# Unit 3's first token-mixing layer and its normalisations on GpSimd instead of VectorE, under a new plan of the instruction order

## The reference

```python
x = x + gated_scan(_layernorm(x))      # i, f, o = sigmoid(x@W+b), s = tanh(x@W+b); h = f*h + i*s; then o*h + x, normalised, *gamma + beta
x = x + mixing(_layernorm(x))          # the first token-mixing layer
x = x + attention(_layernorm(x))       # 16 heads of 16 channels, causal over 4096 tokens
x = x + mixing(_layernorm(x))          # the second token-mixing layer

def mixing(x):
    x_prev = x shifted by one token
    xr = mu_r * x + (1.0 - mu_r) * x_prev
    xk = mu_k * x + (1.0 - mu_k) * x_prev
    return sigmoid(xr @ W_r.T) * (square(relu(xk @ W_k.T)) @ W_v.T)
```

## Time and profile before

| | |
|---|---|
| median of 3 runs | 1678.7 us (1675.02 to 1678.71) |
| profiled execution, its own time | 1679.5 us |
| its span in the profile | 1677.8 us, granted clock 0.994 of full speed |
| TensorE busy | 1625.4 us, 97% |
| VectorE busy | 1511.0 us, 90% |
| ScalarE busy | 1308.5 us, 78% |
| GpSimd busy | 940.3 us, 56% |

### The profile page before, as it was taken

One profiled execution on the slowest core, in us unless ns is written; L12 is line 12 of the kernel. 1 busy time (PEld: TensorE's weight loads), 2 busy tenths in 40 slices (PEclk: granted clock), 3 DMA queues, 4 the chain that ended last, 5 costly groups with the idle time before them and its releaser, 6 DMA issues.

```text
span 1677.8 us, 50396 instructions
## 1 busy us (share of the span) xinstructions
PE 1625.4 (97%) x20458; PEld 663.6 (40%) x20458; DVE 1511.0 (90%) x2905; ACT 1308.5 (78%) x2590; POOL 940.3 (56%) x1295
## 2 busy tenths in 40 slices
PE   8999999999999999999999999999999999999997
PEld 6656444444434344343443332333333332332214
DVE  6868998988999999999999999999999999999603
ACT  2535587667778877888878888988888999888994
POOL 3358878897995798768584534553523520425101
PEclk9999999999999999999999999999999999999999
DMA  4143223113122121131130110103110000000000
GB/s 110 46 90 59 50 56 61 47 42 63 46 45 52 33 52 31 28 57 40 31 59 10 27 33 8 32 19 66 20 25 9 25 8 20 15 14 15 9 1 14
DMA packets 127767, 61.59 MB, mean 37 GB/s; under 512 B 78512, under 2 KB 127536, under 8 KB 127536
## 3 DMA queue, kind: packets, MB, share of 16 engines
q1 hardware_dynamic: 125296, 57.33, 15.7%
q10 hardware_dynamic: 2240, 1.05, 0.4%
HBM read 25.31 MB, written 16.52 MB: 25 GB/s over the span
## 4 chain that ended last, share of the span: by engine, by line
PE 46%; DVE 41%; ACT 5%; POOL 4%; issue 4%; DMA 1%; ACTq 0%; POOLq 0%; DVEq 0%
DVE span_max L2088 34%; PE psum L2442 13%; PE psum L2397 8%; PE psum L2421 8%; PE psum L2168 4%; PE psum L2178 4%; PE psum L2149 3%; PE psum L2157 2%; ACT probs L1744 2%; DVE span_max L2082 1%; ACT probs L1733 1%; DVE small L1930 1%; DVE rows L2020 1%; PE psum L2451 1%; PE psum L2404 1%
## 5 line engine op out<-in xcount | busy, mean ns | idle before, releaser
L2088 DVE TENSOR_REDUCE span_max<-psum 128x1 f32<-128x512 f32 (+1 forms) x2048 | 1237.0, 672 | 35.1 <-PE psum L2397 28.1
L1733 ACT ACTIVATE probs<-psum 128x512 f32<-128x512 f32 (+3 forms) x1788 | 881.1, 568 | 173.0 <-PE psum L2421 169.7
L2397 PE MATMUL psum<-k_stack,q_stack 48*128 48x512 f16 (+3 forms) x2304 | 570.8, 364 | 8.8 <-DVE span_max L2088 5.3
L2421 PE MATMUL psum<-q_stack,k_stack 50*128 50x512 f16 (+3 forms) x2304 | 542.5, 364 | 8.9 <-ACT probs L1744 2.5
L2442 PE MATMUL psum<-probs,v_aug 128*17 128x512 f32 (+3 forms) x3968 | 486.1, 562 | 5.2 <-POOL probs L1569 3.8
L2421 PEld LDWEIGHTS psum<-q_stack,k_stack 50*128 50x128 f16 x2304 | 149.1, 93 | 399.9 <-ACT probs L1733 222.6
L2397 PEld LDWEIGHTS psum<-k_stack,q_stack 48*128 48x128 f16 x2304 | 168.7, 93 | 250.1 <-DVE span_max L2088 165.3
L1569 POOL TENSOR_SCALAR_AFFINE_SELECT probs<-probs 128x512 f32<-128x512 f32 x116 | 74.3, 644 | 182.5 <-ACT probs L1744 115.1
L1733 ACT ACTIVATE w_gates<-psum 128x512 f32<-128x512 f32 (+1 forms) x254 | 130.7, 573 | 17.0 <-PE psum L2421 16.8
L2442 PEld LDWEIGHTS psum<-probs,v_aug 128*17 128x17 f32 x3968 | 67.9, 95 | 119.5 <-issue 96.7
L1562 POOL TENSOR_TENSOR rows<-rows 128x512 f32<-128x512 f32 x26 | 33.2, 1275 | 141.0 <-ACT rows L1674 141.0
(11 more groups left out here) (242 smaller groups left out, 1905.3 us busy)
## 6 DMA issues: line engine op xcount, KB each, us to landing
q_stack<-q_parts SPq DMA_DIRECT2D x192, 32.0 KB, 2.0
k_stack<-k_parts SPq DMA_DIRECT2D x42, 128.0 KB, 4.8
rows<-in_x SPq DMA_DIRECT2D x16, 256.0 KB, 2.9
q_parts<-rows SPq DMA_DIRECT2D x32, 128.0 KB, 1.9
...
```

The costliest lines, as they stand in the source:

```text
L1733: act.activation(probs_of(tile)[:, i, q0:], bank(b)[:, q0:], ACT.Exp, scale=SCALE / QK_SCALE).then_inc(exp_done, 1)
L2088: nc.vector.tensor_reduce(span_max[:, s % SPAN_RING, row:row + 1, k0 // SPAN:k0 // SPAN + 1], bank(b)[:, 0:k1 - k0], AX.X, ALU.max).then_i ...
L2397: ins = nc.tensor.matmul(bank(b)[:, at:at + k1 - k0], q_stack[row:row + SCORE_ROWS, s % Q_RING, v, qt * P:(qt + 1) * P], k_stack[row:row + ...
L2421: nc.tensor.matmul(bank(b)[:, q0:], k_stack[row:row + STACK, g * PAIRS + u, j * P:(j + 1) * P], q_stack[row:row + STACK, s % Q_RING, u, q0 ...
```

## The change

One condition is changed, so that unit 3 leaves VectorE: its four layer norms (before the scan, inside it, before the mixing layer and before the attention) and its first mixing layer. The gated scan of unit 3 stays on VectorE.

```diff
 EARLY = 4
+MIXED_FROM = 3
 LATE = 2
...
 def at_ends(u, ln):
-    return u >= UNITS - LATE if ln == LAST else u < EARLY
+    return u >= UNITS - LATE if ln == LAST else u < MIXED_FROM
```

```diff
-         "dve": (-0.708182031, -15.8951964, 1.56327716, 3.03122896, 3.00215546, 3.03122896, 1.71856018, 2.60387184,
+         "dve": (3.63918768, 1.79871535, 1.79871535, 1.57086866, 7.61597661, 5.55265664, 1.74462935, 1.97922519,
...
-    "DVE": {"ao.scale": 860, "g.max": 602, "g.clip": 75, "h.clip": 1170, "h.scale": 4415, "g.scale": 1890, "qk.scale": 1680, "w.lo": 662, "ones.late": 200, "ln.stats": 660, "ln.mean": 154, "is": 602, "scan": 1615, "y": 671, "z": 600, "mixk": 790, "mixr": 790,
-            "r*kv": 605, "q.part1": 790, "kk.part1": 790, "x3": 600, "neg": 175, "part0": 90, "part1": 195,
-            "recip": 164, "norm": 331, "halve": 300, "prepare": 1950, "halve.v": 336, "scale.bound": 2870, "scale.apply": 2800,
+    "DVE": {"ao.scale": 860, "g.max": 602, "g.clip": 75, "h.clip": 1170, "h.scale": 4415, "g.scale": 1890, "qk.scale": 1680, "w.lo": 760, "ones.late": 200, "ln.stats": 660, "ln.mean": 154, "is": 602, "scan": 1800, "y": 850, "z": 600, "mixk": 950, "mixr": 950,
+            "r*kv": 605, "q.part1": 790, "kk.part1": 790, "x3": 600, "neg": 175, "part0": 260, "part1": 300,
+            "recip": 164, "norm": 331, "halve": 300, "prepare": 1950, "halve.v": 336, "scale.bound": 2870, "scale.apply": 2800,
...
-LANDS_AT = {("store_x2", 1): 5500, ("store_x2", 2): 6500, ("x1.turn", 4): 5200, ("load_q", 0): 3600, ("load_q", 1): 3600}
+LANDS_AT = {("store_x2", 1): 3500, ("store_x2", 2): 4000, ("x1.turn", 4): 4000, ("load_x", 5): 5500, ("load_x", 6): 3500,
+            ("load_q", 0): 6500, ("load_q", 1): 5500, ("load_q", 2): 3800, ("shift.turn", 1): 3500}
```

```diff
-                        sp.wait_ge(spilled_shift, 16 * (s - 1))
+                        sp.wait_ge(spilled_shift[s % 2], 16 * (s // 2))
```

More of the change, by code:

```diff
@@ L236 @@
     "SP": {"ff.turn": 2480, "a.turn": 2480, "load_ao": 500, "load_r": 500, "load_kf": 500, "load_vf": 500, "units.late": 200, "x1.turn": 2480, "x3.turn": 2480, "load_x": 500, "store_x2": 500, "store_q": 1000, "store_k": 1000, "load_k": 2800, "load_q": 2550,
-           "load_x2": 500, "store_out": 500, "shift.turn": 1300, "shift.spill": 400, "place": 900}}
+           "load_x2": 500, "store_out": 500, "shift.turn": 1150, "shift.spill": 400, "place": 700}}
 TURNED = 1300
 LANDS = {"ff.turn": TURNED, "a.turn": TURNED, "load_ao": 5000, "load_r": 5000, "load_kf": 5000, "load_vf": 5000, "units.late": 2500, "x1.turn": 2300, "x3.turn": TURNED, "load_x": 2700, "store_x2": 2200, "store_q": 2000, "store_k": 2000, "load_k": 6200, "act.load_k": 3500,
-         "load_q": 2400, "load_x2": 2700, "store_out": 2200, "shift.turn": 1300, "shift.spill": 1900, "place": 2200}
+         "load_q": 2400, "load_x2": 2700, "store_out": 2200, "shift.turn": 1500, "shift.spill": 1300, "place": 1400}
 PRODUCT = 650
@@ L1010, in build @@
             sem(n) for n in ("squared", "sums_read", "clipped", "powered", "w_scaled", "w_qk_scaled", "w_hi", "w_lo"))
-        a_lo, a_turned, ao_loaded, ao_scaled = (sem(n) for n in ("a_lo", "a_turned", "ao_loaded", "ao_scaled"))
+        a_lo, a_turned, ao_loaded = (sem(n) for n in ("a_lo", "a_turned", "ao_loaded"))
         hi_ready = sem("hi_ready")
@@ L1050, in build @@
         span_reduced = sem("span_reduced")
-        neg_ready, part_ready, shift_ready, turned_shift, spilled_shift = (
-            sem(n) for n in ("neg_ready", "part_ready", "shift_ready", "turned_shift", "spilled_shift"))
+        neg_ready, part_ready, shift_ready = (sem(n) for n in ("neg_ready", "part_ready", "shift_ready"))
+        turned_shift, spilled_shift = ([sem(f"{n}_shift{b}") for b in range(2)] for n in ("turned", "spilled"))
         shift_placed = [sem(f"shift_placed{b}") for b in range(2)]
@@ L1824, in _ @@
                         ins = nc.vector.tensor_scalar(cols[:, COL[name], :], cols[:, COL[name], :], by, None, ALU.mult)
-                    ins.then_inc(qk_scaled, 1)
+                    ins.then_inc(raw_scaled, 1)
                 elif op[0] == "ones.late":
@@ L1887, in _ @@
                 elif op[0] == "qk.scale":
-                    dve.wait_ge(qk_scaled, 1)
+                    dve.wait_ge(raw_scaled, 1)
                     settle(nc.vector.reciprocal(w_power[:, PLAIN:PLAIN + 2], qk_scale))
@@ L1899, in _ @@
                     nc.vector.tensor_scalar(weights["aq"][:], weights["aq"][:], v_back, None,
-                                            ALU.mult).then_inc(ao_scaled, 1)
+                                            ALU.mult).then_inc(raw_scaled, 1)
                 elif op[0] == "w.lo":
@@ L2099, in _ @@
                     if s >= 2:
-                        dve.wait_ge(turned_shift, 16 * (s - 1))
+                        dve.wait_ge(turned_shift[s % 2], 16 * (s // 2))
                     if s == 0:
@@ L2297, in _ @@
                         if u == 0:
-                            pe.wait_ge(qk_scaled, 1)
+                            pe.wait_ge(raw_scaled, 1)
                         if u == SPLIT_FROM:
@@ L2340, in _ @@
                         else:
-                            pe.wait_ge(ao_scaled, 1)
+                            pe.wait_ge(raw_scaled, 2)
                             pe.wait_ge(aT_ready, u - (UNITS - LATE) + 1)
```

69 lines of the change are left out of this document (36 added, 33 removed), and 99 rows, old and new, of the table WORTH.

## The result

The kernel after takes 1698.7 us (median of 4 runs, 1696.45 to 1700.23) against 1678.7 for the one before: ratio 1.0126, 95% interval 1.0112 to 1.0139, slower by 20 us. I had forecast 1671, and the range ended at 1690. The profiled executions lie 17 us apart (1696.45 and 1679.5), their spans 16.6.

What follows compares the result with a forecast made beforehand. VectorE and TensorE were both taken as nearly full, with GpSimd's pace setting VectorE's wait at chunk 2. 1679.5 + 5 - 4 - 9 = 1671.5 on the profiled execution, so 1671 us against the median; range 1657 to 1690.

Steps and rivals of the forecast that it cites:

- +5 at chunk 2: At the 161st reduction, chunk 2's first: 5 us late, from GpSimd's 5 and TensorE's 3, which do not add.
- GpSimd's 5: From 117 us to the 161st reduction: GpSimd's 144.2 us of work with 6% gaps needs 153.4, late by about 5.
- The second place of the order: At the 49th reduction, chunk 1's first: no later than 176 us, with unit 3's keys just ahead of it.
- -4 given back behind chunk 2: Behind the 161st reduction: TensorE has 7 us less to do, of which 4 reach the end.
- -9 from waits that a better plan removes: VectorE's 28.1 us of waits for maxima scores: corrected planner costs remove a third, 9 us, from between 0 and 20.
- 14 would prove me wrong: Between 265.8 and 558 us: the forecast is wrong if the waits for scores stay at 14 us.
- the tail: Behind the last reduction: should stay 98 us, with the same matmuls there; the forecast is wrong if it moves.
- VectorE's lighter start: Ahead of the first reduction: 7.1 us of VectorE's work leave, counted as 0 gain with a bound of 7.
- The fourth rival: Between 117 and 265.8 us: GpSimd holds up VectorE's two-input work, 5.6 us; 1682 us, chance 0.08.
- The third: At the 161st reduction: GpSimd becomes the bound for chunk 2, 15 us late, 4 back; 1687 us, chance 0.20.
- Theory B: Experiments' hypothesis, whole kernel: the new order costs the time; the move alone stays within 6 us of before.

Runs made afterwards that it cites:

- new_order_vector: The kernel after in its own order, but unit 3's norms and first mixing layer back on VectorE: 1698.6 us.
- earlier_49th: The kernel after with pieces moved ahead in its order: chunk 1's first query load, first four scores for maxima and their reductions: 1702.6 us.
- more_tensor: 192 repeated matmuls added in unit 7's gate products, between the 49th and 161st reductions: 1705.8 us on the kernel after, 1692.8 on the kernel before.
- short_unit6: The kernel after with unit 6's gate products on 16 of 256 columns: 1698.2 us.
- four_jobs_behind: The kernel before with four TensorE jobs (96 matmuls) moved from ahead of the 161st reduction's first score to behind the 169th score: 1683.4 us.
- eight_jobs_behind: The kernel before with eight TensorE jobs (192 matmuls) moved from ahead of the 161st reduction's first score to behind the 169th score: 1690.1 us.

## Why the prediction was wrong, step by step

Between the two profiled executions the sum was +5 - 4 - 9. The traces have +17.8 at the 161st reduction, +0.4 from there to the last and -1.6 behind it: 16.6 us.

**"+5 at chunk 2" was mis-sized: 17.8, and its larger part is the term that I had made small.** I had priced TensorE's jobs that are pulled ahead of the 161st at 7 us, taken off 4 for idle time that the new plan would fill, and then let it vanish behind GpSimd's 5. TensorE's busy time up to the 161st grew by 15.7 us, and its idle time did not shrink but grew from 17.8 to 19.9: nothing was filled. Some 3.5 us of the 15.7 are the net loss of the clock, so about 12 are jobs that I had priced at 7. Busy time is not work alone, so the 12 are no more than near: behind the 161st TensorE has 158 matmuls less on record and the same busy time (1294). With unit 3 on VectorE in the new order it is the same (busy for 17.9 more).

**GpSimd's 5 rested on a misread wait.** I took VectorE's 4.15 us ahead of the 161st for GpSimd's pace. SyncE had issued the keys' load by 253.3 us, and stood for VectorE's own shifts. GpSimd's work from 117 us to the 161st was priced well (145.0 us for 144.2, by the windows view of 117 to 283.7), and its gaps were 13%, not the 6% that I chose. Yet VectorE does not wait for its keys at that place in either kernel, and new_order_vector, without unit 3 on GpSimd, has the 161st at 285.0.

**A step without a term in the sum.** The second place of the order showed that all 48 reductions of chunk 0 would stand ahead of unit 3's keys. I drew from it only that the 49th "should come no later than 176 us". Behind a unit's keys come their store, their load and the load of queries; with no reductions left, VectorE must stand through most of that. It did: 20.4 us from the keys' end (162.5) to the 49th, 10.1 of them idle, and the 49th at 182.9. A price stood in the earlier trace rows, 17.6 us from 248.2 to 265.85, though 5.2 of that were SyncE's wait for VectorE. This gap is where 6.6 of the 17.8 us are first seen, but it is not by itself the loss: earlier_49th closed 5.8 us of it and gained nothing. Three things end there nearly together: the loads, VectorE's own queue, and TensorE, which from the first reduction to the 49th is busy for 7.2 us more than before and idle for 0.9 only (3.5 before).

What share each has of the 17.8 us is not settled. Work added to TensorE is felt nearly in full (more_tensor), but work taken from it brought nothing (short_unit6, four_jobs_behind, eight_jobs_behind), and less of GpSimd's brought 5.0 us, most of them by way of TensorE's clock.

**"-4 given back behind chunk 2": nothing came back.** From the 161st to the last reduction the kernel before takes 1313.3 us and after 1313.7, and all kernels with either order in place behind the 161st take 1312 to 1318, whatever was lost ahead of it. TensorE's 7 us less to do there bought nothing. The reason stands in the windows view: VectorE is busy for 1279 us of these 1314 in both kernels, with the same reductions, so less work of TensorE has next to nothing to shorten. And 192 more matmuls ahead of it in the old order were paid nearly in full.

**"-9 from waits that a better plan removes": none.** Over the whole span the waits for scores, masked ones counted in both, rose from 33.6 to 45.6 us. Between 265.8 and 558 us they are 14.1 us, where I had said that 14 would prove me wrong; by the same count they were 16.4 there before. One wait did go, the 4.15 us ahead of the 161st, and others came. Costs nearer to the measured ones did not make a better plan here.

**Right:** VectorE's work (-8.6 for -9.4), GpSimd's (+14.9 for +17.8), nearly the tail (96.2 for 98, though I had said it would stay), and that VectorE's lighter start gains nothing: the first reduction is at 119.8 us after 117.8, which also misses the 110 to 117 that I had named. The fourth rival's price did not come either: the 30 scans by line 2020 took 946 ns on average after 1063. (The mixing instructions' means, 541 and 582 ns, can't be compared, for unit 3's four, 1073 ns each, are no longer among them.)

**The rivals.** The third came nearest, with 15 us late at the 161st and 1687 us, but by luck: its mechanism, VectorE waiting there for GpSimd's keys, is not in the trace, and its 4 back did not come. In the old order the move does cost 7 us, through VectorE's waits for GpSimd's rows ahead of the 49th. Theory B holds: the order costs the 20. Which of the planner's numbers makes it so stays open, for they can't be changed one by one without another order.
